# Gathers of a deformable convolution: items of three taps in the first and last chunk, and a shorter index chain

## What is computed

```
x = x + relu(batchnorm(deform_conv(gn(x))))      # 3x3, 128 to 128 channels
x = x + conv3x3(gn(x)) + bias

deform_conv(v):
  om   = conv3x3(v, w_offset) + b_offset         # 27 channels: 9 dy, 9 dx, 9 mask
  py   = y + dy + ky - 1;  px = x + dx + kx - 1  # a sampling point for each of 9 taps
  cols = bilinear(v, py, px) * sigmoid(mask)     # four corners, zero outside the image
  out  = sum over taps and channels of w_conv * cols + b_conv
```

## Time and profile before

| | us |
|---|---|
| median of three runs | 1347.87 (1346.81 to 1349.62) |
| the profiled execution, its own time | 1352.25 |
| its span, first to last instruction | 1350.5 |
| first gather issued | 19.02 |
| first gather of chunk 2 | 118.53 |
| first gather of the last chunk | 1182.88 |
| last DVE instruction of the last item begins | 1236.53 |

### The profile page before, as it was taken

How to read it: one execution, slowest core, us unless ns; L and a number is a source line. 1 busy time by engine, 2 the same in 40 slices (tenths; PEclk the granted TensorE clock), 3 DMA queues, 4 the chain that set the end, 5 groups by cost and what they waited for, 6 DMA issues and landing times.

```text
span 1350.5 us, 10771 instructions
## 1 busy us (share of the span) xinstructions
PE 794.5 (59%) x2356; PEld 376.7 (28%) x2356; DVE 714.4 (53%) x2687; ACT 373.7 (28%) x1061; POOL 669.0 (50%) x731
## 2 busy tenths in 40 slices
PE   5726535646655535655655635556656555666999
PEld 3312212212122212212222212212122122235777
DVE  3618437446347446446346437446346345386674
ACT  3313214223213214323213214213213223243311
POOL 4464474373373374373373374373373373352643
PEclk8657767777776766767766767766766766656999
DMA  7464463363363463363363473363363463452011
GB/s 262 133 185 116 118 204 109 108 197 110 114 201 103 117 195 110 115 196 109 116 200 104 116 203 111 107 201 107 113 202 102 117 197 103 120 148 63 36 53 53
DMA packets 55828, 181.50 MB, mean 134 GB/s; under 512 B 10964, under 2 KB 11220, under 8 KB 55380
## 3 DMA queue, kind: packets, MB, share of 16 engines
q0 software_dynamic: 51840, 169.91, 43.1%
q1 hardware_dynamic: 3780, 10.52, 2.1%
q10 hardware_dynamic: 144, 0.39, 0.1%
HBM read 176.06 MB, written 4.72 MB: 134 GB/s over the span
## 4 chain that ended last, share of the span: by engine, by line
PE 26%; another core or an unknown queue 23%; DVE 23%; issue 20%; ACT 8%; DMA 0%; DVEq 0%; ACTq 0%
DVE PA L757 11%; PE OMT L348 8%; ACT PA L551 6%; DVE acc L757 5%; PE CO L385 5%; PE TP L395 4%; PE TP L469 2%; PE PA L469 2%; PE CO L469 2%; PE OMT L469 1%; PE VU L469 1%; PE CO L374 1%; DVE bst L686 1%; DVE wt L717 1%
## 5 line engine op out<-in xcount | busy, mean ns | idle before, releaser
L295 POOL DMA_INDIRECT g<-corner_table,idx x648 | 612.8, 946 | 610.4 <-DVE idx L709 392.3
L757 DVE SCALAR_TENSOR_TENSOR PA<-g,wt,PA 128x128 f32<-128x128 f32 x1296 | 366.9, 349 | 489.2 <-ACT PA L551 296.4
L395 PE MATMUL TP<-ident,acc 128*128 128x128 f32 x648 | 166.2, 370 | 420.3 <-DVE acc L757 213.4
L385 PE MATMUL CO<-cols,wcs 128*128 128x384 f32 (+1 forms) x504 | 275.2, 641 | 111.9 <-issue 81.9
L531 ACT ACTIVATE cols<-TP 128x384 f32<-128x384 f32 (+1 forms) x252 | 110.8, 440 | 771.5 <-remote 383.7
L395 PEld LDWEIGHTS TP<-ident,acc 128*128 128x128 f32 x648 | 91.8, 177 | 562.7 <-DVE acc L757 275.0
L757 DVE SCALAR_TENSOR_TENSOR acc<-g,wt,PA 128x128 f32<-128x128 f32 x648 | 195.3, 342 | 76.3 <-DVE acc L757 47.7
L348 PE MATMUL OMT<-xn,woff 128*27 128x384 f32 (+2 forms) x450 | 233.3, 678 | 2.8 <-ACT xn L488 2.1
L551 ACT ACTIVATE PA<-g,wt 128x128 f32<-128x128 f32 x648 | 205.9, 358 | 2.2 <-DMA g<-corner_table,idx 1.8
L385 PEld LDWEIGHTS CO<-cols,wcs 128*128 128x128 f32 x504 | 114.7, 280 | 144.3 <-issue 125.0
L348 PEld LDWEIGHTS OMT<-xn,woff 128*27 128x27 f32 x450 | 56.7, 141 | 180.0 <-issue 176.3
(11 more groups left out here) (120 smaller groups left out, 494.6 us busy)
## 6 DMA issues: line engine op xcount, KB each, us to landing
g<-corner_table,idx POOLq DMA_INDIRECT x648
out_dram<-x SPq DMA_DIRECT2D x16, 288.0 KB, 2.1
x<-x_dram SPq DMA_DIRECT2D x3, 1152.0 KB, 6.1
x<-x_dram SPq DMA_DIRECT2D x2, 384.0 KB, 4.8
wconv<-wconv_dram SPq DMA_DIRECT2D x1, 576.0 KB, 5.0
w<-w_dram SPq DMA_DIRECT2D x1, 576.0 KB
x<-x_dram ACTq DMA_DIRECT2D x1, 384.0 KB, 4.6
grid<-grid_dram SPq DMA_DIRECT2D x1, 162.0 KB, 4.2
```

Source lines behind the costliest of these rows:

```text
L295: pl.indirect_dma_start(out=g[:, k, t].rearrange("p q c -> p (q c)"), out_offset=None, in_=tab_d, in_offset=bass.IndirectOffsetOnAxis(ap=i ...
L385: nc.tensor.matmul(co_bank(c, tiles[0])[:, lo:hi], wcs[:, c // CHUNKS % 2, k, :], cols[:, s % 2, lo:hi], start=False, stop=(k == TAPS - 1) ...
L395: last = nc.tensor.transpose(TP[s % 2][:, t * P:(t + 1) * P], acc[:, s % 3, t, :], ident[:])
L757: nc.vector.scalar_tensor_tensor(acc[:, s % 3, t, :] if q == 3 else a, g[:, k, t, q, :], wt[:, c % 2, q, t, k:k + 1], a, ALU.mult, ALU.add ...
```

## The change

- `items`: in the first and last chunk an item is now three taps of one tile (9 items; the last chunk has 10, since its last tile is cut 3, 3, 2, 1). A unit of such an item has its own place in the PSUM bank, in `acc` and in `cols`; the product is issued once a unit, the copy once an item.
- `gathered[i]` is now counted by the item's place in the chunk. No place comes twice in a chunk, so POOL waits within the first chunk only for the indices of tiles 1 and 2, and within the last only for the readers of the chunk before.
- Preparing chunk 1 now stands at items 0 to 7 of chunk 0, as in all chunks.
- `indices`: the constant of the rounding is folded into `grid`, and clamps are done on the value with that constant added. The chain to the indices is four instructions deep (six are issued, with two independent pairs). The fraction is kept negated, which puts scalar_tensor_tensor in the place of tensor_tensor in three places. The indices of tiles 1 and 2 are computed right after those of tile 0.
- Start: image 0 in four loads (1, 1, 2 and 2 chunks) alternating between SP and ACT; 14, 2 and 7 warm-up products before, between and after the two group products; ACT normalises its second part before it copies the offsets, and scales item 0 after the offsets of tiles 1 and 2.
- End: tiles 1 and 2 of the last chunk have own slots in the last aggregation.

```diff
-        return [(k, (t,)) for t in range(TILES) for k in range(TAPS)]
-    return [(k, tuple(range(TILES))) for k in range(TAPS)]
+TAP_SETS = ((0, 1, 2), (3, 4, 5), (6, 7, 8))
+LAST_SETS = ((0, 1, 2), (3, 4, 5), (6, 7), (8,))
...
+        return [[(k, t) for t in range(TILES)] for k in range(TAPS)]
+    return [[(k, t) for k in taps] for t in range(TILES) for taps in (LAST_SETS if (c, t) == (ALL - 1, TILES - 1) else TAP_SETS)]
...
-    k, tiles = items(c)[i]
-    return 16 * (c * TILES + max(tiles) + 1)
+    return 16 * sum(len(items(e)[i]) for e in range(c + 1) if i < len(items(e)))
...
+X0 = (0, 1, 2, 4, CHUNKS)
...
-                for i, (k, tiles) in enumerate(items(c)):
-                    if c in BY_TILE and tiles[0]:
-                        if c == 0 and tiles[0] == 1 and k == 0:
-                            pl.wait_ge(idx_ready, 2)
-
-                        pl.wait_ge(lerped, tiles_before(c, i - TAPS + 1) * LERP)
-                    elif c:
-
-                        pl.wait_ge(lerped, tiles_before(c - 1, last_use(c - 1, k, tiles) + 1) * LERP)
-                    for t in tiles:
+                for i, units in enumerate(items(c)):
+                    if c == 0 and i == len(TAP_SETS):
+                        pl.wait_ge(idx_ready, 2)
+                    if c:
+
+                        used = max(last_use(c - 1, unit) for unit in units)
+                        if i < len(items(c - 1)):
+                            used = max(used, i)
+                        pl.wait_ge(lerped, units_before(c - 1, used + 1) * LERP)
+                    for k, t in units:
...
-                        ).then_inc(gathered[k], 16)
+                        ).then_inc(gathered[i], 16)
...
+                runs = [(k, t, P) for k, t in units] if c in BY_TILE else [(units[0][0], 0, CP)]
...
+                for n, (k, t, size) in enumerate(runs):
+                    if k == 0:
+                        conv_shift(c, t, t * P, t * P + size)
+                    if n == 0:
+                        pe.wait_ge(copied, s + 1)
+                    last = nc.tensor.matmul(co_bank(c, t)[:, t * P:t * P + size], wcs[:, c // CHUNKS % 2, k, :], cols[:, s % 2, n * P:n * P + size],
+                                            start=False, stop=(k == TAPS - 1))
+                last.then_inc(conved, 1)
...
-            warm_up(11)
+            warm_up(14)
             group_mean(0)
+            warm_up(2)
             group_var(0)
+            warm_up(7)
...
-            act.dma_start(x[:, HW // 3:2 * HW // 3], x_d[:, 0, HW // 3:2 * HW // 3]).then_inc(x0b_in, 16)
+            for i in (1, 3):
+                act.dma_start(x[:, X0[i] * CP:X0[i + 1] * CP], x_d[:, 0, X0[i] * CP:X0[i + 1] * CP]).then_inc(x0_in[i], 16)
...
+            norm_xn(0, 1)
             act.wait_ge(wo_in, 32)
             copy_offsets(0, 0, TILE_ROWS * W)
-            norm_xn(0, 1)
             masks(0, 0, 1)
             norm_xn(0, 2)
+            copy_offsets(1, TILE_ROWS * W, CP)
+            masks(1, 1, TILES)
+            copy_u(0)
             act.wait_ge(wt_ready, 1)
-            copy_offsets(1, TILE_ROWS * W, CP)
-            scale_tap(0, 0)
-            scale_tap(0, 1)
-            masks(1, 1, TILES)
+            scale_item(0, 0)
             scale_weights(0)
-            copy_u(0)
             copy_v(0)
-            copy_cols(0, 0)
...
+                nc.vector.scalar_tensor_tensor(low[:, n], ot[:, n, 0:18], -0.5, grid[:, j, n], ALU.add, ALU.add).then_inc(index_step, 1)
+                nc.vector.scalar_tensor_tensor(pos[:, n], grid[:, j, n], -ROUND, ot[:, n, 0:18], ALU.add, ALU.add).then_inc(index_step, 1)
+                dve.wait_ge(index_step, s + 1)
+                nc.vector.tensor_scalar(low[:, n], low[:, n], ROUND - 1.0, ROUND + H - 1.0, ALU.max, ALU.min).then_inc(index_step, 1)
+                dve.wait_ge(index_step, s + 2)
+                nc.vector.tensor_scalar(pos[:, n], pos[:, n], -1.0, float(H), ALU.max, ALU.min).then_inc(index_step, 1)
+                dve.wait_ge(index_step, s + 3)
+                nc.vector.tensor_scalar(row[:, n], low[:, n, 0:9], -ROUND, float(SIDE), ALU.add, ALU.mult).then_inc(index_step, 1)
+                dve.wait_ge(index_step, s + 5)
+                nc.vector.scalar_tensor_tensor(idx[:, c % 2, n], low[:, n, 9:18], float(b * TABLE + SIDE + 1) - ROUND, row[:, n], ALU.add, ALU.add).then_inc(idx_ready, 1)
+                nc.vector.scalar_tensor_tensor(less_frac[:, n], low[:, n], -ROUND, pos[:, n], ALU.add, ALU.subtract).then_inc(index_step, 1)
...
             indices(0, 0, 0, 1)
+            indices(0, 1, 1, TILES)
```

192 lines of the change are left out of this document (88 added, 104 removed).

## The result

The changed kernel takes **1333.36 us** (median of 6 runs, 1331.31 to 1338.18) against 1347.34 us (6 runs, 1344.65 to 1351.68) for the kernel before in the same session: ratio 0.9899, 95% interval 0.9873 to 0.9925. It is 14 us faster, where 29 were forecast, and 1319 stood against 1333. The profiled execution is its fastest, 1331.31 us, with a span of 1329.6; that of before, 1352.25 us, was 4.9 us above this median. So 20.9 us lie between the two spans and 14.0 between the medians.

A forecast was written before the change was run, and what follows sets the result against it. No engine bounds it: hand-overs between engines slow late in each burst of gathers, and POOL waits in a tail. 10.3 (start, chunk 0) + 14.1 (index chain) + 4.5 (last chunk) = 28.9 us off: 1319 us, range 1304 to 1337.

The forecast's parts named there:

- The index chain's own term: Last link before POOL's gathers: 0.67 us shorter in each of 21 cycles, gain 14.1 us (0 to 19).
- Rival 1: Index gain swallowed because recovery from the slowdown ends the tail: gain 14.8 us in all, 1333 us, chance 0.17.
- The start: Before the first gather: 1.8 us from the offset product, 0.7 from the index chain; first gather at 16.5 us.
- rival 3: PE's clock stays low and seven warm-ups delay the offset product: loss of 3 us, 1324 us, chance 0.05.
- chunk 0: Without POOL's holds chunk 1 starts at 60.5 us, chunk 2 at 108.2: gain 10.3 us, the start's 2.5 included.
- The last chunk: First gather to last lerp, 21 gathers in a row: 49.5 us in place of 54.0, gain 4.5 (-1 to 10).
- behind the last item nothing changes: End of the last chunk: one-tap item, copy and statistics stay as before, cost 0.
- Rival 4: Unthrottled gathers slow the hand-overs: chunk 1 at 70 (+5), last chunk +3, index gain swallowed; 1356 us, chance 0.05.

The follow-up runs named there:

- e2: The kernel before with only the new start (four loads, 14, 2 and 7 warm-ups, order of ACT's first steps): 1346.8 us, ratio 0.996.
- e1: The kernel before with only the new index chain (the constant in grid): 1328.2 us, ratio 0.983.
- e4: The changed kernel, POOL holding each item i>2 of chunk 0 until item i-3 is lerped: 1325.4 us, ratio 0.980.

## Why the prediction was wrong, step by step

- **The index chain's own term held.** The mean over 20 chunks from the first of its instructions to the indices is 1.36 us before and 0.68 after. The timeline of the DVE at the end of chunk 1, against the earlier trace rows:

```profile
114.96 0.21 DVE L708 SCALAR_TENSOR_TENSOR low<-OMT,grid 128x54 f32<-128x54 f32 x1 [0.21 <-PE OMT L361]
...
115.65 0.19 DVE L717 SCALAR_TENSOR_TENSOR idx<-low,row 128x27 int32<-128x27 f32 x1
```

  The cycles gained more, 1.04 us between the two kernels and 0.92 between e2 and e1, which ran on one chip: 19.3 us in 21 cycles, at the bound of 19 that the forecast gave for a shorter instruction list. The rest came before item 4's end. Why is open. Rival 1 (the gain is swallowed) is out, though its time, 1333 us, is the one measured: that is luck, since it has no gain in the cycles and 14.8 us in the first two chunks and the last, and the profiled pair has a gain of 21.9 in the cycles and a loss of 1.0 in all the rest. One thing that rival 1 saw is there: in the 21 cycles of the kernel before, the second new item ends anywhere from 30.7 to 39.6 us after the chunk's first gather, and the third always at 42.5 to 42.9, some 9 us after the last gather. What sets the third item's time is thus the end of the burst and not the item before it; the chain, which comes two items later, still counts in full.
- **The start held**: first gather 16.17 for 16.5, offset product 2.37 us for 2.1, and rival 3 is out. The window of the earlier trace rows now reads a granted clock of 1.00, the 2.4 GHz level, with PE busy for 3.88 of 5 us and not 2.88:
```profile
10.00:15.00 5.00, 3.88 (x31) 3.05 (x29) 0.82 (x5) 2.89 (x5) 0.00 (x0) 1.00 0.50 157
```

  The Trainium skill ("TensorE: Matmul & The Clock Gate", the part on the HAM clock gate) says that a busy PE gets the full clock, and this row agrees.
- **The step that failed is chunk 0**: "Then six items could pass in a burst as in the middle". The middle's six are four old items, whose gathers have landed, and two new. In the changed kernel's cycles the old ones end 4 to 14 us after the first gather, before the hand-overs get slow, and of the new ones 1.55 are done at the burst's end (the kernel before has 1.4, so "two" was read too high as well). Chunk 0 has only new ones, which wait for their own gathers: two passed before it got slow, and the third by 49.6 us. Chunk 1 came at 69.0 and not 60.5, chunk 2 at 116.1 and not 108.2, a gain of 2.4 for 10.3. With one hold (e4) chunk 1 comes at 61.7, and 1.0% of the time comes back. The stretch from there to chunk 2 went as forecast, -5.9 for -5.2. Taking POOL's holds away was costed as a gain; it was the loss.
- **The last chunk failed the same way**, +1.7 for -4.5: 21 gathers in a row, ACT idle 11.6 us. The forecast's own count, four or five items left at 41.5 us, gave 52 to 54, and that count held; but the sum took 49.5, between it and the 44 of no slowdown. Five were left, and the first of them ended only at 46.7 us, which makes 55.7. And "behind the last item nothing changes" cost 1.2 us: the product that stands before the last transpose, that of the item two before the last, has three taps.
- **Rival 4** named the mechanism, put the point of decision at fewer than three of chunk 0's items by 50 us and gave chunk 1 at 70 and the last chunk +3; measured were three, 69.0 and +1.7. It had 0.05, for "a middle burst passes six items", the same mistake. Its time, 1356, was wrong because it also let the index gain be swallowed, which was another rival's matter: with that gain left in, it reads 1356 - 14 = 1342 against 1333, and the rest is mostly that chunk 1 took 5.9 us back.
- The sum of the profiled pair, 20.9 for 28.9, hides half of it: everything before chunk 2 is short by 7.9 us, all behind the last chunk's first gather by 7.9, and the cycles are over by 7.8. Part of that is that one execution of before 4.9 us above its median stands against one of after 2 us below. The medians say 14.0.

## What to carry to other kernels

Where a stretch gets slow under its own load, ask how much of what is new passes in it, not how much passes in the steady state. A wait that a change removes may be what paces the work: where unbroken indirect gathers and slow hand-overs stand side by side in a timeline, try a hold or a pause in the issuing queue before shortening anything else; the pause was worth 14% on the changed kernel, where the index chain was worth 1.7% on the one before. And time such a thing on more than one chip: with four clears after every three gathers the changed kernel took 15% less than the kernel before on one chip, and the kernel before 19% more than itself on another.

## What the runs showed of the hardware

- In unbroken bursts of 27 indirect DMAs from POOL, one every 1.25 us (0.95 busy and 0.30 between), hand-overs between PE, ACT and the DVE came late from some 15 us into the burst, and ACT idled 16.7 us or more at once before a copy, in every such profile from the sessions in which the kernel before takes 1350 us. Taking bytes (53 for 208 GB/s), rows (64 for 128) or PE's work out did not end it. A pause of 1.16 us after every third did (longest idle 2.8 us), and so did a hold that let at most 9 follow each other (3.6 us). The instructions themselves kept their durations, 349 and 350 ns for a lerp with and without pauses. The Trainium skill ("Perfetto Trace Analysis", the per-engine timelines) says that semaphore waits and their propagation lie outside the windows that the profile draws; this trace agrees, in that the lateness appears only as idle time, "remote" or "issue". The Trainium skill also has a rule by which DVE and GpSimd exclude each other at a shared port ("Trainium Architecture — The Big Picture", "What this means for kernel authors"). That alone would not make ACT wait for PE, as it does in these rows; and no run here shows such a lock. What does delay the hand-overs is open.
- The same program takes 1350 us on four chips and 965 on another, there with all seven runs within 0.3% of each other, in one session. Why is open too.
